# A second-order feature interaction tower: layer 1's squares as one 128-row fp32r product, and the gram scratch laid out by blocks of eight fields

## The reference

```python
def _L0_rec_ref(input, W0, b0, W1, b1, W2, b2):
    x_vec = input
    outs = []
    for W, b in params:
        z = jnp.einsum('bhd,bfd->bhfd', x_vec, input)
        B, h, f, d = z.shape
        z = z.reshape(B, h * f, d)
        x_vec = jnp.einsum('oc,bcd->bod', W, z) + b[None, :, None]
        outs.append(x_vec.sum(axis=2))
    return jnp.concatenate(outs, axis=1)
e = jnp.stack([tbl_0[ids[:, 0]], tbl_1[ids[:, 1]], ..., tbl_63[ids[:, 63]]], axis=1)
z = _L0_rec_ref(e, L0_rec_W0, L0_rec_b0, L0_rec_W1, L0_rec_b1, L0_rec_W2, L0_rec_b2)
h = jnp.concatenate([z, dense_ctx], axis=1)
h = jnp.maximum(h @ W_top1 + b_top1, 0.0)
h = jnp.maximum(h @ W_top2 + b_top2, 0.0)
y = h @ W_top3
```

## Time and profile before

| | |
|---|---|
| median of 3 runs | 1180.73 us (1180.33 to 1181.44) |
| the profiled execution, its own time | 1183.49 us |
| its span | 1181.5 us, 13928 instructions |
| granted TensorE clock, mean | 0.994 of 2.4 GHz |
| TensorE matmul / weight load busy | 1117.9 / 745.3 us |
| VectorE / ScalarE / GpSimd busy | 997.4 / 681.9 / 905.2 us |
| DMA | 142.87 MB, mean 121 GB/s; 294 and 297 GB/s in slices 38 and 39 of 40 |

### The profile page before, as it was taken

The page is one execution under the profiler, slowest core; times in us unless marked ns, Lnnn a source line. Parts: engine busy times, 40 slices in busy tenths (PEclk is TensorE's granted clock), DMA queues, the critical chain, the costliest instruction groups (busy, mean ns, idle before and its releaser), DMA issues.

```text
span 1181.5 us, 13928 instructions
## 1 busy us (share of the span) xinstructions
PE 1117.9 (95%) x4276; PEld 745.3 (63%) x4276; DVE 997.4 (84%) x652; ACT 681.9 (58%) x695; POOL 905.2 (77%) x403
## 2 busy tenths in 40 slices
PE   0499999999999999999999999999999999999998
PEld 0256666666666666676666666666666666667685
DVE  4589899989998989899899989898998999896542
ACT  5256465665656656656656566566566665654533
POOL 6459998889988888888899888888898996575000
PEclk9999999999999999999999999999999999999999
DMA  6542424234252524252342525241523425242991
GB/s 240 170 130 65 113 74 150 65 120 121 77 155 74 157 74 140 68 152 66 109 131 71 160 74 157 74 140 64 146 76 104 136 69 160 73 152 94 294 297 46
DMA packets 103836, 142.87 MB, mean 121 GB/s; under 512 B 11745, under 2 KB 55009, under 8 KB 103042
## 3 DMA queue, kind: packets, MB, share of 16 engines
q1 hardware_dynamic: 95618, 140.42, 39.3%
q0 software_dynamic: 8192, 2.11, 2.2%
HBM read 114.96 MB, written 27.53 MB: 121 GB/s over the span
## 4 chain that ended last, share of the span: by engine, by line
PE 83%; POOL 4%; issue 3%; DMA 3%; SPq 2%; ACT 2%; DVE 1%; ACTq 0%
PE acc L1085 50%; PE acc L1079 26%; POOL z_lo L580 3%; PE turn_gram_ps L1153 3%; DMA z_float<-gram_scratch 2%; PE acc L1108 1%; POOL emb L571 1%; ACT x L878 1%; DMA z<-gram_scratch 1%; PE z_ps L1214 1%; PE turn_gram_ps L1140 1%; DMA land<-x_scratch 1%; ACT z_hi L1046 0%; DVE z_lo L816 0%; SPq L512 0%
## 5 line engine op out<-in xcount | busy, mean ns | idle before, releaser
L580 POOL TENSOR_TENSOR z_lo<-z,z_hi 128x2048 fp32r<-128x2048 f32 x143 | 659.5, 4613 | 116.8 <-ACT z_hi L849 110.3
L1085 PE MATMUL acc<-z_hi,w_hi 128*128 128x512 f32 x896 | 379.0, 423 | 6.8 <-DVE z_lo L659 4.2
L1079 PE MATMUL acc<-z_float,w_sb 128*128 128x512 f32 x768 | 349.1, 601 | 8.2 <-ACT x L878 7.6
L1085 PE MATMUL acc<-z_hi,w_lo 128*128 128x512 f32 x896 | 354.6, 396 | 0.0
L1085 PE MATMUL acc<-z_lo,w_hi 128*128 128x512 f32 x896 | 354.3, 395 | 0.0
L849 ACT ACTIVATE z_hi<-z 128x2048 fp32r<-128x2048 f32 x144 | 275.1, 1910 | 53.6 <-DVE z L647 53.6
L571 POOL DMA_INDIRECT emb<-in_tables,rows_chunk x256 | 245.4, 959 | 63.3 <-issue 51.8
L1079 PEld LDWEIGHTS acc<-z_float,w_sb 128*128 128x128 f32 x768 | 144.4, 191 | 174.6 <-issue 166.4
L858 ACT ACTIVATE z_hi<-z_ps 128x1024 fp32r<-128x1024 f32 x160 | 164.9, 1031 | 135.9 <-PE acc L1085 108.9
L659 DVE TENSOR_TENSOR z_lo<-z_ps,z_hi 128x1024 fp32r<-128x1024 f32 x160 | 194.9, 1218 | 45.3 <-ACT z_hi L858 45.3
L647 DVE TENSOR_TENSOR z<-operand_even,x_shift 128x2048 f32<-128x2048 f32 x80 | 183.0, 2287 | 37.3 <-PE acc L1085 16.6
(11 more groups left out here) (112 smaller groups left out, 640.7 us busy)
## 6 DMA issues: line engine op xcount, KB each, us to landing
land<-x_scratch SPq DMA_DIRECT2D x128, 256.0 KB
land<-x_scratch SPq DMA_DIRECT2D x128, 128.0 KB
x_shift<-x_scratch SPq DMA_DIRECT2D x16, 1024.0 KB, 5.8
gram_scratch<-gram SPq DMA_DIRECT2D x32, 512.0 KB
x_shift<-x_scratch SPq DMA_DIRECT2D x16, 768.0 KB
z_float<-gram_scratch SPq DMA_DIRECT2D x7, 1024.0 KB, 10.8
x_scratch<-emb SPq DMA_DIRECT2D x32, 192.0 KB
x_shift<-gram_scratch SPq DMA_DIRECT2D x6, 1024.0 KB, 9.2
```

The costliest lines, as they stand in the source:

```text
L580: pool.tensor_tensor(z_lo[:, slot], z[:, slot], z_hi[:, slot].bitcast(F32), ALU.subtract).then_inc(subtracted, 1)
L1079: mm = pe.matmul(acc[:, :], weights[:, tile0 + q, :], z_float[:, g.float_slot(pos), q, :], start=start and q == 0, stop=stop and q == QUAD ...
L1085: mm = pe.matmul(acc[:, :], w[:, tile, :], zz[:, slot, q, :], start=False, stop=stop and n == 2)
```

## The change

Two edits that have nothing to do with each other.

The first: the squares are computed twice by ScalarE, once rounded to fp32r into rows 0 to 63 of `z_sq`, once in float32 into rows 0 to 63 of `x1` (free at that time); VectorE subtracts one from the other into rows 64 to 127 of `z_sq` (`split_square`). The weights get the same: `w_sq[:, 0]` is the rounded weight in all 128 rows, `w_sq[:, 1]` its low part in rows 0 to 63 and zero below. Two fp32r matmuls of 128 rows then give high x high + low x high and high x low. They stand behind layer 1's split unit and no longer in front of the first plain unit.

The second: in HBM `gram_scratch` is laid out (hidden, field block, half chunk, 8 fields x 16 samples), no longer (hidden, half chunk, 64 fields x 16 samples). A store now writes 8 pieces of 512 B for each partition, not one of 4 KB; a load reads one piece of 8 KB, not 16 of 512 B.

```diff
-    gram_scratch = nc.dram_tensor("gram_scratch", (HID, 2 * CHUNKS, FIELDS, HALF_B), F32, kind="Internal").ap()
+    gram_scratch = nc.dram_tensor("gram_scratch", (HID, HALF_BLOCKS, 2 * CHUNKS, F_BLOCK * HALF_B), F32, kind="Internal").ap()
...
-        z_sq = sb("z_sq", [FIELDS, COLS])
+        z_sq = sb("z_sq", [P, COLS], F32R)
+        w_sq = sb("w_sq", [P, 2, HID], F32R)
...
                 if m == LAND_SLOTS:
-                    waits.append((squared, c.count(1, 1)))
+                    waits.append((squared, c.count(2, 2)))
...
             def store_gram(c, half):
-                offset, = at(c.count(2 * FIELDS * HALF_B, half * FIELDS * HALF_B))
+                offset, = at(c.count(2 * F_BLOCK * HALF_B, half * F_BLOCK * HALF_B))
                 wait_all((gram_staged, c.count(BLOCKS, 2 * half + 2)))
                 sp.dma_start(bass.AP(gram_scratch.tensor, offset,
-                                     [[2 * CHUNKS * FIELDS * HALF_B, HID], [1, FIELDS * HALF_B]]),
-                             gram[:, :, :].rearrange("p f b -> p (f b)")).then_inc(gram_stored, 16)
+                                     [[2 * CHUNKS * FIELDS * HALF_B, HID], [2 * CHUNKS * F_BLOCK * HALF_B, HALF_BLOCKS],
+                                      [1, F_BLOCK * HALF_B]]),
+                             gram[:, :, :].rearrange("p (k f) b -> p k (f b)", f=F_BLOCK)).then_inc(gram_stored, 16)
...
-                sp.dma_start(gram_buffers[k % GRAM_BUFFERS].rearrange("p c f b -> p c (f b)"), bass.AP(
-                    gram_scratch.tensor, (half * CHUNKS * FIELDS + fb * F_BLOCK) * HALF_B,
-                    [[2 * CHUNKS * FIELDS * HALF_B, HID], [FIELDS * HALF_B, CHUNKS], [1, F_BLOCK * HALF_B]],
+                sp.dma_start(gram_buffers[k % GRAM_BUFFERS].rearrange("p c f b -> p (c f b)"), bass.AP(
+                    gram_scratch.tensor, (fb * 2 + half) * CHUNKS * F_BLOCK * HALF_B,
+                    [[2 * CHUNKS * FIELDS * HALF_B, HID], [1, CHUNKS * F_BLOCK * HALF_B]],
...
+            dve.memset(w_sq[FIELDS:P, 1, :].bitcast(F32), 0.0).then_inc(w_sq_split, 1)
+            dve.wait_ge(w_sq_rounded, 1)
+            dve.tensor_tensor(w_sq[0:FIELDS, 1, :], w0_sb[0:FIELDS, L1_PLAIN, :], w_sq[0:FIELDS, 0, :].bitcast(F32),
+                              ALU.subtract).then_inc(w_sq_split, 1)
...
+            def split_square(c):
+                dve.wait_ge(squared, c.count(2, 2))
+                dve.tensor_tensor(z_sq[FIELDS:P, :], x1[0:FIELDS, :], z_sq[0:FIELDS, :].bitcast(F32),
+                                  ALU.subtract).then_inc(square_split, 1)
...
                 layer1(nxt, 0)
+                split_square(nxt)
                 layer1_middle(nxt)
...
             def square(c):
                 if not c.is_(0):
-                    act.wait_ge(used, layer1_group(c.plus(-1)).count(4, 1))
-                act.activation(z_sq[:, :], land[0:FIELDS, layer1_group(c).land_slot(0), :], ACT.Square).then_inc(squared, 1)
+                    act.wait_ge(used, layer1_group(c.plus(-1)).count(4, 3))
+                    act.wait_ge(square_split, c.count(1))
+                if not (c.is_(0) or c.is_(1)):
+                    act.wait_ge(sum1_ready, c.count(1))
+                    act.wait_ge(x1_stored, c.count(32))
+                src = land[0:FIELDS, layer1_group(c).land_slot(0), :]
+                act.activation(z_sq[0:FIELDS, :], src, ACT.Square).then_inc(squared, 1)
+                act.activation(x1[0:FIELDS, :], src, ACT.Square).then_inc(squared, 1)
...
+            act.wait_ge(w0_summed, L1_PIECES + len(PLAIN_PIECES))
+            act.activation(w_sq[:, 0, :], w0_sb[:, L1_PLAIN, :], ACT.Copy).then_inc(w_sq_rounded, 1)
...
             def layer1(c):
                 g = layer1_group(c)
-                pe.wait_ge(squared, c.count(1, 1))
                 if not c.is_(0):
                     pe.wait_ge(x1_ready, c.count(1))
-                pe.matmul(acc1[:, :], w0_sb[0:FIELDS, L1_PLAIN, :], z_sq[:, :], start=True, stop=False)
-                float_unit(g, acc1, w0_sb, 0)
+                float_unit(g, acc1, w0_sb, 0, start=True)
                 split_unit(g, 1, acc1, 0)
+                pe.wait_ge(square_split, c.count(1, 1))
+                for part in range(2):
+                    pe.matmul(acc1[:, :], w_sq[:, part, :], z_sq[:, :], start=False, stop=False)
                 halves_unit(g, acc1, QUAD)
                 float_unit(g, acc1, w0_sb, QUAD, pos=3, stop=True)
...
-    squares[0:FIELDS] = w0[:, np.arange(FIELDS) * (FIELDS + 1)].T
+    squares[0:FIELDS] = squares[FIELDS:P] = w0[:, np.arange(FIELDS) * (FIELDS + 1)].T
```

More of the change, by code:

```diff
@@ L292, in build @@
         wt2_sb = land[:, 0:2, :].rearrange("p a (h n) -> p (a h) n", h=2)
-        h1, h2, y_sb = z_float[:, 0], z_float[:, 1], z_sq[0:1, :]
+        h1, h2, y_sb = z_float[:, 0], z_float[:, 1], x2t[0:1, :]
         acc1 = ps("acc1", [P, COLS])
@@ L326, in build @@
         landed = [sem(f"landed_{s}") for s in range(LAND_SLOTS)]
-        copied, squared = sem("copied"), sem("squared")
+        copied, squared, square_split = sem("copied"), sem("squared"), sem("square_split")
+        w_sq_rounded, w_sq_split = sem("w_sq_rounded"), sem("w_sq_split")
         formed = sem("formed")
@@ L754, in _ @@
             layer1(c0, 0)
+            split_square(c0)
             dve.wait_ge(rounded, 1)
@@ L762, in _ @@
             layer1(c1, 0)
+            split_square(c1)
             layer1_middle(c1)
@@ L862, in square @@
                 if not c.is_(0):
-                    act.wait_ge(used, layer1_group(c.plus(-1)).count(4, 1))
-                act.activation(z_sq[:, :], land[0:FIELDS, layer1_group(c).land_slot(0), :], ACT.Square).then_inc(squared, 1)
+                    act.wait_ge(used, layer1_group(c.plus(-1)).count(4, 3))
[6 more added lines that the diff above has]
+                act.activation(x1[0:FIELDS, :], src, ACT.Square).then_inc(squared, 1)
             def take_x1(c):
                 act.wait_ge(used, layer1_group(c).count(4, 4))
-                if not c.is_(0):
+                if c.is_(0):
+                    act.wait_ge(square_split, 2)
+                else:
                     act.wait_ge(x1_stored, c.count(32))
@@ L1175, in _ @@
             pe.wait_ge(w0_summed, L1_PIECES + len(PLAIN_PIECES))
+            pe.wait_ge(w_sq_split, 2)
             pe.wait_ge(w_split, L1_PIECES)
```

## The result

The changed kernel takes 1163.97 us (median of 4 runs, 1161.76 to 1164.91) where the kernel before takes 1181.09 (4 runs, 1180.33 to 1181.76): ratio 0.9852, interval 0.9839 to 0.9864, 17.1 us less. The forecast was 1162.0, range 1159.4 to 1170.5. The profiled execution took 1163.56 us with a span of 1161.6 and a granted clock of 0.997.

A forecast was written before the change was run, and what follows sets the result against it. TensorE's queue was taken to bound about 100 to 1094 us, gram DMA loads the end; squares -11.1, loads -7.9, start +0.3 sum to -18.7 us, from 1180.73 to 1162.0 us, range 1159.4 to 1170.5.

The forecast's parts named there:

- The squares on TensorE: Layer 1: squares fall from 1.26 us a chunk to 0.47 as two fp32r matmuls, saving 0.79 us.
- 14 chunks, 11.1 us: Layer 1 of the 14 chunks after the first two saves 0.79 us each, 11.1 us in all.
- I put all this at nothing; its cover is those 2.8 us twice: Layer 1: added ScalarE and VectorE work, 1.3 us delay, costs nothing; operands have 2.8 us to spare in two places.
- The stores in 512 B pieces, nothing: Gram stores, two a chunk: 1.8 us each at the 512 B load rate, 10 us of cover, no cost.
- Rival 5: Slower: 512 B gram stores hold up the shift loads queued behind; 1198 us at 14 us a store; chance 0.03.
- The loads: Gram loads at the end: 2.81 us per MB instead of 3.56, TensorE becomes the bound, 7.9 us saved.
- Rival 2: Gram loads gain nothing, HBM or the 128 KB partition pitch setting 3.56 us; 1169.9 us; chance 0.10.
- The start, +0.3: Second chunk at the start: VectorE's added subtraction shows on the chain, costing 0.3 us, bounds nothing and 1.3.
- The sum: Whole kernel: -11.1 - 7.9 + 0.3 = -18.7 us, giving a median of 1162.0 us.
- savings are taken off both alike: Whole kernel: the same savings come off the profiled execution, 1183.49 us, and the median, 1180.73, 2.8 us lower.
- The signs named: Expected profile: squares' matmuls about 0.4 us, 64.3 us a chunk, end rounds of 2.9 us a block ended by TensorE.
- No wait of TensorE for VectorE or GpSimd in the steady part: Expected profile, steady part: TensorE never waits for VectorE or GpSimd.

The follow-up runs named there:

- experiment 4: Kernel before, with its plain float32 matmul of the squares made over 128 rows, the lower 64 zeros; 1175.95 us, ratio 0.9954.
- run 9: Changed kernel, subtraction of the squares made five times, raw squares after the second chunk in PSUM, TensorE waiting ahead of layer 1; 1191.88 us, ratio 1.0069.
- experiment 10: Changed kernel, VectorE's one subtraction of the squares moved two products later, into GpSimd's low part; 1177.83 us, ratio 0.9957.
- Experiment 1: Kernel before with the new gram layout alone, squares as before; 1173.41 us, ratio 0.9933.
- run 6: Changed kernel with VectorE's subtraction of the squares made five times, each waiting for the one before; 1273.74 us, ratio 1.0754.
- run 8: Kernel before with another gram layout: loads in 4 pieces of 2 KB a partition, stores in 512 B; 1177.04 us, ratio 0.9939.

## Why the prediction was right, step by step

- **The squares on TensorE**: right in mechanism and nearly in size. Forecast 0.79 us a chunk, measured 0.775 (65.055 to 64.280); the new pair is the 0.47 us of the forecast. What I had put down to going from 128 rows to 64 and back, experiment 4 gives a number: 0.38 us in the period, 0.19 in the matmul itself and the rest around it.
- **14 chunks, 11.1 us**: 10.1 came. 14 times 0.775 is 10.85; the other 0.7 us were lost in the last round, to one subtraction that took 3.83 us.
- **"I put all this at nothing; its cover is those 2.8 us twice"**: the result holds in all rounds but the last, the reason doesn't. The cover is 1.6 to 1.8 us a round (experiments 9 and 10), and in experiment 10 what it ends at is GpSimd: the step said that ScalarE's delay doesn't reach it, which is so for the low part of layer 1 and not for the next one. There GpSimd can give 2.3 us a round and no more; TensorE feels it as a wait for ScalarE's gram copy. I had asked when the operands of layer 1 are wanted, not what else is behind work of VectorE in the round. The change adds 0.69 us to VectorE there, so it was far enough from any of these numbers. The step also priced the subtraction by its size; that the price depends on what GpSimd does at the time was missing altogether, and it was luck of the place that 13 of 14 rounds have gathers there: two products later, the change would have lost some 12.5 of its 17 us.
- **The stores in 512 B pieces, nothing**: right. Experiment 1 has them in every round, and the period stays 65.06. Rival 5 falls with it.
- **The loads**: 2.81 us a load was taken, 2.48 came; it made little difference, since I had TensorE as the next bound at 2.93 us a block and 3.45 for a plain one, and there it stopped. 7.9 forecast for the stretch, 8.1 measured, 8.0 for the layout alone. (The working counts 287 steps to the last matmul of the twelve blocks where there are 286; that is 0.1 us.) Rival 2 falls: the partition pitch of 128 KB is still there, and 423 GB/s come over it. The line rate from 512 B up of the Trainium skill, "DMA: Bandwidth & Descriptors", table at its head, is now gainsaid on the very tensor: 295 GB/s in pieces of 512 B, some 390 in 2 KB, 423 in 8 KB.
- **The start, +0.3**: open. The scatter there is 3 us from run to run, and nothing in the runs resolves 0.3.
- **The sum**: 1162.0 against 1163.97. Of the 2.0 us, 0.4 is the base, which four runs put at 1181.09 and not 1180.73; 1.0 is the shortfall in the rounds, less 0.2 gained at the end; the last 0.8 is smaller than the scatter of the start and stays unplaced. The profiled execution of before was 2.4 us above its median, that of after 0.4 below its own, so "savings are taken off both alike" holds only to about the scatter of the start.
- **The signs named**: 64.3 us a chunk, matmuls of 0.395 us, rounds of 2.93 us ended by TensorE, all seen. "No wait of TensorE for VectorE or GpSimd in the steady part" held too. The wait in the last round was for ScalarE.

## What to carry to other kernels

Cover isn't the distance to the next consumer of the operand that is made later; it is the shortest such distance over everything queued behind the work on each engine that it delays, the waits of the other engines in that round with it, and one run with a known extra piece of work measures it better than reading does. Before adding an elementwise operation to VectorE, look where its operands lie: with both in SBUF, its price depends on GpSimd's timeline at that very moment, and a trace in which 15 of 16 calls are short says nothing of a place two instructions on. When a run with added work comes out far too slow, read its granted clock first: part of the loss may be the clock that fell behind the wait. And when a stage is paced by loads, work out what paces it next before valuing the faster load: here 2.81, 2.66 or 2.48 us a block would all have given the same end.

## What the runs showed of the hardware

- A VectorE subtraction of 64x512 with both inputs in SBUF takes 0.685 us beside GpSimd's gathers, and beside GpSimd's low part (4.6 us, all in SBUF) it ends 0.55 to 0.57 us after that ends: 3.00, 3.83 and 5.25 us in the three rows shown. With one input in PSUM it took 0.683 to 0.687 us in 70 of 70 calls.
- A float32 matmul of 512 columns over 64 rows, set between matmuls of 128 rows, costs 0.38 us a time more than the same over 128 rows with zeros below.
- Gram loads of 1 MB over a partition pitch of 128 KB: 3.56 us in pieces of 512 B, 2.66 to 2.71 in 2 KB, 2.48 in 8 KB.
- In run 6 the granted clock fell in every round; behind a wait of TensorE of 3.80 us it was 0.50 (466.70 to 472.70 us); two pieces of the chain took 3.2 us more for it.
- The granted clock dipped in run 8 (0.89, then 0.77 in two stretches of 5 us) while TensorE had no idle time at all in its row, nor in the 20 us ahead of it, and it cost 1.7 us; run 9 has such a dip too, in the same part of the program, where the work turns from split to plain matmuls.
